# Another order of the sync engine's work inside an attention step, and rows of ones written elsewhere

## The reference

```python
scores = jnp.einsum('bhqd,bhkd->bhqk', q, k) * scale
attn = jax.nn.softmax(scores, axis=-1)
out = jnp.einsum('bhqk,bhkd->bhqd', attn, v)
...
x = x + _L0_xattn_ref(_layernorm(x, axis=-1), ctx_1024, ctx_1024)
x = x + _L0_ffn_ref(_layernorm(x, axis=-1), L0_ffn_w_gate, L0_ffn_w_up, L0_ffn_w_down)
```

## Time and profile before

| what | us |
|---|---|
| median of 3 runs | 541.68 |
| lowest and highest run | 538.37, 542.48 |
| the profiled execution, its own time | 540.0 |
| span of its instructions | 538.2 |
| attention, first scores of step 0 to those of step 1 | 33.5 to 53.8 |
| steps 1, 2, 3 and 4 | 17.3, 14.8, 14.4, 15.9 |
| steps 5, 6 and 7 | 14.2, 14.2, 14.3 |

### The profile page before, as it was taken

How to read it: one execution, slowest core, us unless ns; L and a number is a source line. 1 busy time by engine, 2 the same in 40 slices (tenths; PEclk the granted TensorE clock), 3 DMA queues, 4 the chain that set the end, 5 groups by cost and what they waited for, 6 DMA issues and landing times.

```text
span 538.2 us, 13724 instructions
## 1 busy us (share of the span) xinstructions
PE 492.4 (91%) x4036; PEld 382.7 (71%) x4036; DVE 442.3 (82%) x1129; ACT 371.2 (69%) x739; POOL 306.0 (57%) x424
## 2 busy tenths in 40 slices
PE   1885999999999999999776799999999999999996
PEld 0232556556566666655445699999999999999996
DVE  3786799899998999988444789888899888899764
ACT  5355798989998999977663465666656665656653
POOL 7636566646556565533415565667666667666543
PEclk9999799999999999999876999999999999999999
DMA  7749658666667666530000000000000000000000
GB/s 213 221 131 234 185 141 226 191 174 185 185 184 186 187 196 196 154 102 22 3 0 2 0 12 21 19 19 19 10 19 19 19 19 19 10 19 21 22 22 29
DMA packets 49985, 48.97 MB, mean 91 GB/s; under 512 B 4768, under 2 KB 47648, under 8 KB 49952
## 3 DMA queue, kind: packets, MB, share of 16 engines
q1 hardware_dynamic: 49952, 48.58, 31.9%
HBM read 18.94 MB, written 4.19 MB: 43 GB/s over the span
## 4 chain that ended last, share of the span: by engine, by line
PE 72%; DVE 7%; SPq 5%; issue 5%; DMA 4%; POOL 3%; ACT 3%; DVEq 0%; POOLq 0%; ACTq 0%
PE SC L1172 21%; PE PV L1172 12%; PE PV L1120 9%; PE MX L1102 9%; PE SC L1088 8%; DVE MF L776 4%; PE T L1197 4%; SPq L299 3%; DMA QS<-MT 2%; PE T L1202 2%; PE T L1069 2%; PE T L1037 1%; PE SC L1197 1%; DMA KT<-in_ctx_t 1%; PE T L1044 1%
## 5 line engine op out<-in xcount | busy, mean ns | idle before, releaser
L776 DVE TENSOR_REDUCE MF<-MX 128x2 f32<-128x512 f32 x256 | 165.8, 683 | 20.9 <-PE MX L1102 17.3
L609 ACT ACTIVATE P<-SC 128x512 f32<-128x512 f32 x256 | 140.8, 593 | 26.8 <-PE SC L1088 25.2
L1102 PE MATMUL MX<-KS,QS 96*128 96x256 bf16 x512 | 104.3, 288 | 7.1 <-DVE MF L776 5.3
L1088 PE MATMUL SC<-QS,KS 98*128 98x256 bf16 x512 | 100.9, 280 | 5.9 <-DMA QS<-MT 5.8
L532 POOL TENSOR_TENSOR HQ<-HN,hscale 128x704 f32<-128x704 f32 x31 | 43.1, 1391 | 60.5 <-DVE HN L928 60.5
L1120 PE MATMUL PV<-P,VA 128*32 128x256 f32 x1024 | 72.0, 401 | 0.5 <-ACT OT L618 0.5
L1088 PEld LDWEIGHTS SC<-QS,KS 98*128 98x128 bf16 x512 | 44.2, 99 | 39.0 <-ACT P L609 17.3
L709 ACT ACTIVATE HH<-T 128x768 fp32r<-128x768 f32 x31 | 25.2, 813 | 67.1 <-PE T L1197 67.1
L1102 PEld LDWEIGHTS MX<-KS,QS 96*128 96x128 bf16 x512 | 43.3, 100 | 38.2 <-DVE MF L776 29.1
L1172 PE MATMUL SC<-WH,XH 128*128 128x352 f32 x256 | 68.3, 348 | 0.0
L1172 PE MATMUL SC<-WH,XL 128*128 128x352 f32 x256 | 62.6, 326 | 0.0
(11 more groups left out here) (137 smaller groups left out, 1034.4 us busy)
## 6 DMA issues: line engine op xcount, KB each, us to landing
KS<-KP SPq DMA_DIRECT2D x96, 128.0 KB, 2.9
QS<-QP SPq DMA_DIRECT2D x96, 128.0 KB, 2.4
QN<-in_x_p SPq DMA_DIRECT2D x16, 256.0 KB, 3.0
KT<-in_ctx_t SPq DMA_DIRECT2D x16, 256.0 KB, 3.1
C<-in_ctx SPq DMA_DIRECT2D x16, 256.0 KB, 4.2
X<-in_x SPq DMA_DIRECT2D x16, 256.0 KB, 4.6
out<-OB SPq DMA_DIRECT2D x32, 128.0 KB, 1.7
W<-in_L_ffn_w_down SPq DMA_DIRECT2D x2, 352.0 KB, 3.4
```

The lines of the kernel that those rows point to most:

```text
L609: nc.scalar.activation(P[g % 2][:, j, :, :], SC[h % 3][:, :, :], ACT.Exp, scale=0.25).then_inc(exp_done, 1)
L776: nc.vector.tensor_reduce(MF[st.slot(off, 2)][:, :, h:h + 1], MX[h % 2][:, :, :], AX.X, ALU.max, negate=True).then_inc(mx_done, 1)
L1088: last = nc.tensor.matmul(SC[h % 3][:, k, :], KS[r][0:ROWS, h, k * 128:(k + 1) * 128], QS[r][0:ROWS, h, :], start=True, stop=True)
L1102: last = nc.tensor.matmul(MX[h % 2][:, q, :], QS[r][0:PROD, h, q * 128:(q + 1) * 128], KS[r][0:PROD, h, :], start=True, stop=True)
```

## The change

In each step the sync engine issues the K stack and the copy of maxima first and the loads after them; the Q stack and the weight pieces come last. X is loaded for item t and not t+1. The first `load_first(3, 3)` moves ahead of the steps, and the gate weight pieces of step -1 go ahead of its Q stack. The rows of ones of KS 0 and 1 are both written by GpSimd in step -2, those of KS 2 in step -1 after the first `m_parts`, and those of KS 3 by one ScalarE activation in step -1. VectorE's wait for the down weights moves from position (1, 1) to (3, 3) of step 4.

```diff
@@ -350,16 +350,9 @@
             load_context(0, 0)
             sp.wait_ge(w_zeroed, 4)
             load_blocks(0, wg_in, 0, 2, w_begun)
+            load_first(3, 3)
 
             def attention_step(st):
-                if st.first >= 0 and st.has(RING):
-                    sp.wait_ge(v_ready, st.times(0, 1, 1))
-                    gate(sp)
-                    load_first(st.item(RING), st.slot(RING, RING))
-                if st.first >= 0 and st.has(2):
-                    load_context(st.item(2), st.slot(2, RING))
-                if st.first >= 0 and st.has(1):
-                    load_x(st.item(1), st.slot(1, RING))
                 if st.has(LEAD):
                     r = st.slot(LEAD, RING)
                     sp.wait_ge(k_low, st.times(LEAD, 1, 1))
@@ -373,16 +366,22 @@
                     r = st.slot(1, 2)
                     sp.dma_start(QS[st.slot(1, RING)][PROD:ROWS, :, :].rearrange("d h t -> d (h t)"),
                                  MT[r][:, :]).then_inc(m_stacked[r], 16)
+                if st.first >= 0 and st.has(RING):
+                    sp.wait_ge(v_ready, st.times(0, 1, 1))
+                    gate(sp)
+                    load_first(st.item(RING), st.slot(RING, RING))
+                if st.has(2):
+                    load_context(st.item(2), st.slot(2, RING))
+                if st.has(0):
+                    load_x(st.item(0), st.slot(0, RING))
                 if st.first == -1:
-                    load_first(3, 3)
+                    load_weights(-1)
                 if st.has(LEAD):
                     sp.wait_ge(q_out, st.times(LEAD, 3, 3))
                     gate(sp)
                     stack(QS[r_q(st)], QP[st.slot(LEAD, 2)], (0, 0, 0, 1, 1, 2), r_q(st))
-                if st.first == -1:
-                    load_context(1, 1)
-                    load_x(0, 0)
-                load_weights(st.first)
+                if st.first >= 0:
+                    load_weights(st.first)
 
             def r_q(st):
                 return st.slot(LEAD, RING)
@@ -428,13 +427,11 @@
                 nc.gpsimd.memset(WD[:, r, FI:], 0.0).then_inc(w_zeroed, 1)
             pool.wait_ge(w_zeroed, 4)
 
-            def row_of_ones(r, st):
-
-                pool.wait_ge(k_low, st.first + LEAD + 1)
-                if st.has(1):
-                    pool.wait_ge(v_ready, st.first + 2)
-                nc.gpsimd.memset(KS[r][PROD:ROWS, :, :], 1.0).then_inc(ones_ready, 1)
-                pool.wait_ge(ones_ready, r + 1)
+            def rows_of_ones(rs):
+
+                for r in rs:
+                    nc.gpsimd.memset(KS[r][PROD:ROWS, :, :], 1.0).then_inc(ones_ready, 1)
+                    pool.wait_ge(ones_ready, r + 1)
 
             def attention_step(st):
                 if st.has(-2):
@@ -474,8 +471,13 @@
                     nc.gpsimd.tensor_scalar(VA[r][:, :, :, 0:DK],
                                             C[rc][:, :, :].rearrange("p q (h d) -> p q h d", d=DK),
                                             1.0, 0.0, ALU.mult, ALU.add).then_inc(v_ready, 1)
-                if 1 - LEAD <= st.first < 1 - LEAD + RING:
-                    row_of_ones(st.first + LEAD - 1, st)
+                if st.first == 1 - LEAD:
+                    pool.wait_ge(k_low, 2)
+                    rows_of_ones((0, 1))
+                if st.first == -1:
+                    pool.wait_ge(v_ready, 1)
+                    pool.wait_ge(m_parts, 1)
+                    rows_of_ones((2,))
                 if st.has(GRID):
 
                     ws = wslice(st, GRID)
@@ -655,6 +657,11 @@
                         if (g, j) == (1, 2) and st.has(LEAD):
                             for q in range(QT):
                                 normalise(st, q)
+                        if (g, j) == (1, 2) and st.first == -1:
+                            act.wait_ge(consts, IDENTS)
+                            nc.scalar.activation(KS[RING - 1][PROD:ROWS, :, :].rearrange("d h t -> d (h t)"),
+                                                 ident[PROD:ROWS, 0:1].to_broadcast([ROWS - PROD, H * S]),
+                                                 ACT.Identity, bias=1.0, scale=0.0).then_inc(ones_last, 1)
                         if (g, j) == (2, 0) and st.first < 0:
                             maxima_out(st)
                         for n, at in enumerate(((2, 0), (2, 3), (3, 3))):
@@ -835,7 +842,6 @@
                     dve.wait_ge(w_loaded[0], 32)
                 elif st.first == RING:
                     dve.wait_ge(w_loaded[1], 48)
-                    dve.wait_ge(w_loaded[2], 32)
                 dve.wait_ge(w_scaled, st.times(SCALE, 1))
                 nc.vector.tensor_reduce(wmax[:, :], blocks(wslice(st, SCALE)), AX.X, ALU.max,
                                         apply_absolute_value=True).then_inc(w_seq, 1)
@@ -896,6 +902,8 @@
                             output(st, 1)
                         if (g, j) == ((3, 2) if st.first > 0 else (3, 3)) and st.has(SCALE):
                             weight_inverses(st)
+                        if (g, j) == (3, 3) and st.first == RING:
+                            dve.wait_ge(w_loaded[2], 32)
                         if st.first == B - 1 and HG * g + j < LOTS:
                             weights_out(HG * g + j)
 
@@ -1080,8 +1088,10 @@
                     if st.first == 0:
                         pe.wait_ge(ones_ready, 1)
                         pe.wait_ge(consts, CONSTS)
-                    if st.first in (1, 2, 3):
+                    if st.first in (1, 2):
                         pe.wait_ge(ones_ready, st.first + 1)
+                    if st.first == RING - 1:
+                        pe.wait_ge(ones_last, 1)
 
                 pe.wait_ge(exp_done, st.times(0, H, h - 2 if h > 2 else (0, -2, -1)[h]))
                 for k in range(QT):
```

More of the change, by code:

```diff
@@ L216, in program @@
             ("w_seq", "w_scaled", "w_abs", "w_c", "w_grid", "w_done"))
-        ones_ready = sem("ones_ready")
+        ones_ready, ones_last = sem("ones_ready"), sem("ones_last")
         w_tr, w_out = sem("w_tr"), sem("w_out")
```

## The result

| | before | changed |
|---|---|---|
| median of 20 runs each, us | 538.67 | 534.52 |
| lowest and highest | 535.10, 542.48 | 530.46, 542.95 |
| the profiled execution | 540.0 | 542.95 |

The ratio is 0.9915, with an interval of 0.9888 to 0.9943: 4 to 5 us were won where 12.1 had been forecast. It leaves out three runs of the changed kernel that lie over 1.5% above its fastest (the medians of all 20 give 0.9923), and the profiled one is among them, the longest of its 20. So this trace shows what the change costs at its worst.

What follows compares the result with a forecast made beforehand. TensorE was taken to set the pace of undisturbed attention steps, with longer steps to be won: 1.3 + 1.0 + 4.2 + 2.4 + 0.6 + 0.2 + 1.7 + 0.7 = 12.1 us. From 541.7 that gives 529.6, stated as 529.5, range 525 to 536.

Steps and rivals of the forecast that it cites:

- the copy of item 1 still late: Rival, chance 0.10: queue still busy in step 0, stall above 2 us, clock falls again; 4 to 5 us back, 534.
- The cast: Before step 0: first cast of maxima has no GpSimd memset beside it, 1.46 to 0.17 us; gain 1.3 us.
- the memset gone from step 0: Step 0: VectorE's L851 gets shorter and TensorE's wait of 1.03 us for VectorE goes; gain taken as 1.0 us.
- the copy of item 1: Step 0: copy of maxima issued at 44.45 instead of 47.93, TensorE's stall falls from 4.46 to 0.3; gain 4.2 us.
- The wait of step 4: Step 4: VectorE's 1.84 us wait for down weights goes, step falls from 15.9 to 14.2 us; gain 1.7 us.
- ScalarE's write: Step -1: ones of KS 3 by one activation, 3.5 to 4.3 us; costs nothing, or a few tenths.
- The loads in a usual step: Usual steps: loads go ahead of the Q stack, which slips 0.1 or 0.2 us; no stall taken, bound 0 to 6 us.
- the spare of KT: Usual steps: KT lands 0.15 us before ScalarE reads it at 3.1 us to land, 0.55 us before at 2.7.
- a sign of being wrong: Signs listed: waits at L583 in every step, a copy stall in step 1, a wait for `stacked` at (2, 2).
- steps 1, 2, 3, 4 and 8: Longer attention steps before, 17.3, 14.8, 14.4, 15.9 and 14.9 us; gains claimed 2.4, 0.6, 0.2, 1.7 and 0.7 us.
- KT much late: Rival, chance 0.06: KT loads slower than before in every step, ScalarE waits at (0, 2); 545 to 550 us.
- KT a little late: Rival, chance 0.16: loads land some tenths later, ScalarE delays its exponentials; 0.3 us in 12 steps, 3.6 back, 533.

Runs made afterwards that it cites:

- split: Changed kernel with C and X loaded behind the Q stack, QN and KT still ahead of it; 529.54 and 529.64 us on two chips, both 0.9854.
- issue slots: Changed kernel with C and X each cut in two DMAs, 16 partitions ahead of the Q stack and 112 behind it; 530.73 us, ratio 0.9851.

## Why the prediction was wrong

It gave a gain of 12.1 us, of which 4 to 5 came, and a chance of 0.90 to faster by over 1%; the ratio of 0.9915 is within 1%, to which it gave 0.06. The median of 534.52 lies inside its range of 525 to 536 and beside the 534 of "the copy of item 1 still late". That is luck: the loss came by another mechanism than any that it priced, and the sum was set against a median that was 3.0 us too high. From 538.67 the same sum gives 526.6, 7.9 below what was measured.

**What held.** The cast (1.3), the memset gone from step 0 (1.0) and the copy of item 1 (4.2) make 6.5 us up to the first scores of step 1. They come at 47.4, 47.2 and 47.3 us in the three traces, against 53.8 - 6.5 = 47.3. The wait of step 4 is gone in the full change. ScalarE's write cost nothing.

**What failed first** is one step, "The loads in a usual step": the Q stack's "data queue behind 1 MB of loads. The K stack now has just that ahead of it [...] and nothing stops for it". The second sentence was taken as a proof of the first. I had worked out the spare of KT to 0.15 us and not that of the stack whose wait I named myself, at the end, as a sign of being wrong. Worked out, it is 2.5 us, against 8.9 for the K stack. The median landing rose from 2.4 us to 3.9, to 4.4 to 4.8 in the three stacks before the longest stalls, with 6.0 to 6.7 for their slowest pieces. The issue slipped too, by up to 1.0 us in steps 5 to 9 where 0.1 or 0.2 was forecast, and by 0.7 before the stall of step 10. The term was put at nothing; on the same chip the kernels without the wait are 3.3 us (split) and 2.5 us (issue slots) faster than the changed one.

**That is less than half of what is missing.** The split kernel, with no wait for the Q stack, gains 7.9 us by its ratio of 0.9854, and not 12.1. What else failed is the base of the sum: gains were read from one execution of 540.0 us, 1.3 above the median of its kernel, and the stall of 4.46 us in it is 2.10 to 4.67 in four other traces of the old order. Against that one execution the split kernel is 540.0 - 529.6 = 10.4 us faster. Further, the copies of maxima and KT still cause waits up to step 6 that the sum had at nothing: steps 1 to 13 of the split kernel are 1.3 and 2.6 us longer than the sum left them. What of the 4.2 us remains behind these two is not assigned.

**Where the gain went**, in the traces. The sum of steps 1 to 13 over 14.2 us each was 6.2 us before, of which I took 5.6 as won in steps 1, 2, 3, 4 and 8 (2.4 + 0.6 + 0.2 + 1.7 + 0.7 = 5.6). In the three traces of the changed kernel it is 14.4, 3.9 and 5.7 us; in the two of the split kernel 3.2 and 1.9. So the start brings 6.4 to 6.6 us in every trace of the changed kernel, and the steps behind it bring between -8.2 and +2.3: 540.0 - 6.5 - 2.3 = 531.2 (measured 531.01), 540.0 - 6.6 - 0.5 = 532.9 (533.06), 540.0 - 6.4 + 8.2 = 541.8 (542.95). The 1.1 us that the last sum lacks lie behind attention: from the first scores of step 15 to the end it is 281.7 us there and 280.6 before. The stalls were paid for with the clock too: waits of 1.79, 1.85 and 1.73 us made steps 3.6, 5.0 and 3.3 us longer than 14.2.

**Rivals.** "KT much late" fell. "KT a little late" came, at a smaller price than its 3.6 us: ScalarE's waits for KT are 1.2, 1.7 and 0.8 us in the three traces, and the two steps with the longest, 0.71 and 0.84, take 14.8 and 14.9 us. "The copy of item 1 still late" fell, with 0.4 us in all steps. The 550 of "KT much late" is written as 538.5 + 12, and its own terms are 529.5 + 21 = 550.5. That a part does nothing where it stands alone was no rival of mine, and it is what most of the table shows.

**Open.** By my sum the ones (2.3 us) and the wait (1.7) should bring 4.0 us together, 0.9926; together they bring 0.9923 and alone nothing by the ratios, each with 0.3 to 0.4% of uncertainty on either side. In the traces of either one alone the pieces that I counted are there: the ones alone reach step 1 at 50.8 instead of 53.8, the wait alone has 14.6 us in step 4 instead of 15.9. But these two traces are of the fastest of 12 executions each, 535.23 and 534.41 us, and don't stand for the usual one; and by the medians the ones alone do gain something, 536.88 against 538.34. Why the wait alone shows nothing is not settled. The order, added to the other two, changes the ratio of 0.9923 to 0.9893 to 0.9918, which is within the intervals; split, it adds some 0.7%.

## What to carry to other kernels

Before you move a transfer, write down for every transfer that comes behind it on the queue its last issue, its landing and its first reader; queueing that a transfer with 9 us of slack hides is a stall for one with 2.5. Look for a place where the bytes delay nothing before you clear the one that hurts now: half the loads ahead of the Q stack and half behind were better than all ahead (0.985 against 0.989 to 0.992), though against all behind (0.989, with overlapping intervals) it isn't decided. Read more than one trace, and take the base of a sum from the median of many executions. A change made of parts is to be measured in its combinations, since here the order was 1% slower by itself and stopped costing only beside the other two.

## What the runs showed of the hardware

Stalls of TensorE at its upper clock level, 2.4 GHz, cost their own length or much more. With stalls of 1.16, 1.32 and 1.41 us (the two further traces of the changed kernel) the steps were 15.5, 15.7 and 15.7 us, and with 1.67 us (the kernel with two more loads) 16.1, so 1.3 to 1.9 us over 14.2, at a mean clock of 1.00. With 1.73, 1.79 and 1.85 us (the profile after) they were 17.5, 17.8 and 19.2, with a mean clock of 0.90, 0.90 and 0.82 in them; with 2.06 to 2.35 us (the kernel with two more loads) 17.8 to 18.1, at 0.90 or 0.91. The stall plus the missing share of the clock times the length of the step, 1.73 + 0.10 x 17.5, 1.79 + 0.10 x 17.8 and 1.85 + 0.18 x 19.2, make 3.5, 3.6 and 5.3 us, and the steps were 3.3, 3.6 and 5.0 longer.

A piece of 128 KB landed 2.4 us after its issue with nothing directly ahead of it, and after up to 6.7 us behind 1 MB of loads. The sync engine's own issue can stretch: a piece of the Q stack takes 0.60 us to issue in the middle case, and at most 1.17 in the kernel before, 1.59 in the split and 2.50 in the changed kernel. A transfer that lands earlier can cost time, by way of the memset that it lets go beside a cast, 3.56 us in place of 0.49.

The kernel before gave medians from 536.85 to 539.35 us on five occasions. Its runs on these lay between 534.84 and 544.94 us, the 38 of the changed kernel between 529.92 and 542.95, and the 11 of the split kernel between 528.38 and 532.28. What the queue did differently from one execution to the next is not in these traces.
